# A four-layer network on one Trainium2 core: folding weights at the head of the third expert stage, first down products one slot later

## Chip, cores and metric

The kernel runs on 1 core of one Trainium2 chip. The metric is the device time of one execution in microseconds (us). Before the change it is 2271.5 us, the median of 3 runs (2271.24 to 2273.16).

## What is computed

The reference sends 16 sequences of 56 tokens of width 256 (896 tokens in all) through four layers. Each layer adds a gated cross attention over a context of 1500 rows, and then a gated feed-forward part. Those of layers 0, 2 and 3 are mixtures of experts. The part around the change is the feed-forward part of layer 2, the third of the four feed-forward stages, with 16 experts of which each token takes 6:

```
x = x + tanh(g_xattn[2]) * L2_attention(layernorm(x), context)
h = layernorm(x)
scores = softmax(h @ gate_w.T);  cw = the 6 largest scores of each token, else 0
y = sum over e of cw[:, e] * ((silu(h @ w_gate[e].T) * (h @ w_up[e].T)) @ w_down[e].T)
x = x + tanh(g_ffn[2]) * y
x = x + tanh(g_xattn[3]) * L3_attention(layernorm(x), context)
```

The attention of layer 3 has weights of its own for each of 16 heads (`Wq`, `w_kc_q`, `W_qr`, `W_kr`, `w_kc_kv`, `Wo`). The kernel multiplies them together ahead of the attention ("folds" them), two heads at a time, so that each query is one product with a folded matrix.

## The kernel before

The program is a row of stages. At the end of each, all five instruction queues meet (`stage_end`, semaphore `stage_met`). Every fp32 product is done as three products of high and low parts (`split_pairs`: high by high, high by low, low by high), so that one 128x128 by 448 product is three matmuls of 448 columns, written by line 922. Tokens are taken in two halves of 448.

**The third feed-forward stage** (`FFN[2]`) has 22 blocks of 128 hidden units (16 experts of 176). The order of its work is one hand-built list of tasks, made by `expert_order(22, side)` and walked by all five queues; each takes from it the tasks that are its own. A slot `k` stands for one block and one half of the tokens. In slot `k` the list has:

- `up`: TensorE multiplies the normalised tokens `YH`, `YL` with the gate and the up weights of the block (`WH`, `WL`), 12 matmuls into two banks of psum; ScalarE takes silu of the first (`R`, line 1933) and VectorE multiplies by the second (`HF`, line 2658). The `up` of slot 0 is done in the stage before.
- `gate`: VectorE multiplies `HF` by the tokens' gate for the block's expert (`GB`, line 2673), ScalarE makes the high part (`HH`, line 1956) and GpSimd the low part (`HL`, line 2201). `R`, `HF`, `HH` and `HL` are rings of 4 tiles, so the `HH` of slot `k` waits for the down product of slot `k - 4`.
- `down`: TensorE multiplies `HH`, `HL` with the down weights, 6 matmuls that are added up in banks 0 to 3 of psum over the whole stage. In the steady state slot `k` has the `down` of slot `k - 3`.
- one step of `side`, the folding for the next layer's attention, made by `fold_order(3, 1)`. Its first step is the load of the first pair's weights (`fload`), and then there are four steps a pair: `fu` (line 1180, from `WqrT`; ScalarE copies the result to `U`, line 1708), `fm` (line 1186, from `WoT` and `Wv`; to `MH`, line 1711, and `ML`), `fg` (`U` by `WcT`; to `G`, line 1716) and `fa` (line 1200, `G` by `Wq`; to `AH` and `AL`). There is one set of buffers for these weights, so pair `p + 1` is loaded behind pair `p`.
- `split`: ScalarE and GpSimd make the high and low parts of a coming block's weights (`WH` line 1926, `WL` line 2185) from `WS`, which SP has loaded (`fetch`, line 1052; four buffers).

The products of `up` and of the folding steps go through banks 4 to 7 in turn (`upper_uses`): each use waits until the result four uses back has been taken out. So the first half of `up` of slot 5 waits for `u_set`, ScalarE's copy of the first `fu`.

**The gates** are there only in slot 2: VectorE works the routing out (`route`), TensorE turns it, VectorE copies it to `GT`, SP writes it to DRAM (`gates_scratch`, line 1058), waits until it is there, and then reads it back broadcast, the gates of three blocks in six issues (`gload`, line 1063). SP issues in program order, and waits in that order too. The folding weights of pair 0 (lines 981 to 991, in `sp_fold`) and the `fetch` of block 5 stand behind these six.

Of the kernel before, what the change touches and what calls it, by code (L numbers as in the profile page):

```python
# [20 lines left out]
H = 16  # L21
# [6 lines left out]
NB0, NB2, NB3 = E0 + 4, E2 * I2 // P, E3 + 1  # L28
# [134 lines left out]
def expert_order(blocks, side):  # L163

    slots = [(n, c) for n in range(blocks) for c in range(2)]
    order, free = [("fetch", n) for n in range(4)] + [("split", 0), ("split", 1), ("route", 0)], FFN_FREE[2 if blocks == NB2 else 3]
    side = list(side)
    for k in range(len(slots) + 3):  # L170
        if k < len(slots):
            n, c = slots[k]
            if c == 0 and 4 <= n + 3 < blocks:
                order.append(("fetch", n + 3))
            order.append(("up", n, c))
        if k in (0, 2):
            order.append(("route", 1 + k // 2))
            if k == 2:
                order += [("gload", n) for n in range(free, free + 3)]
        for x in {0: (), 1: (), 2: (), 3: (0,), 4: (1, 2), 5: (3, 4, 5)}.get(k, (k,)):  # L180
            if x < len(slots):
                n, c = slots[x]
                order.append(("gate", n, c))
                order += [("gload", n + 3)] if c == 1 and free <= n < blocks - 3 else []
        for x in {4: (0,), 5: (1, 2)}.get(k, (k - 3,) if k > 5 else ()):
            order.append(("down", *slots[x]))
            if slots[x] == (blocks - 1, 0):
                order += [t for step in side for t in step]
                side = []
                order.append(("back", 0))  # L190
        if k < len(slots):
            n, c = slots[k]
            if side and k >= 2:
                order += side.pop(0)
            if c == 1 and n + 2 < blocks:
                order.append(("split", n + 2))
    return order + [("back", 1)] + ([("make", mt, 0) for mt in range(4, H // 2)] if blocks == NB2 else [])


def folding_ahead():  # L200
# [139 lines left out]
def bit_order(fold):  # L340
# [3 lines left out]
    for k in range(NT + 5):  # L344
# [19 lines left out]
FFN_FREE = {0: NB0 - E0, 2: 0, 3: NB3 - E3}  # L364
SWIGLU = {0: False, 2: True, 3: True}
CORES, CORE0 = {n: core_order(n != 2) for n in (1, 2, 3)}, core0_order()
FFN = {0: sparse_order(context_order(), folding_ahead()),
       2: expert_order(NB2, fold_order(3, 1)),
       3: expert_order(NB3, [])}
FFN1_FOLD = fold_order(2, 1)  # L370
FFN1 = FFN1_FOLD[0] + bit_order(FFN1_FOLD[1:])
# [2536 lines left out]
```

## Time and profile before

| | |
|---|---|
| median of 3 runs | 2271.5 us |
| the profiled execution's own time | 2275.43 us |
| its span in the trace | 2273.6 us |
| mean granted clock of TensorE | 0.97 of full |
| TensorE (PE) busy | 2143.3 us, 94% |
| VectorE (DVE), GpSimd (POOL), ScalarE (ACT) busy | 1541.5, 1478.2, 1035.6 us |
| chain that ended last, share on PE | 81% |
| moved by DMA | 160.14 MB, 70 GB/s mean |

Times in the trace are us from the start of the span, so the profiled execution's own time is 1.83 us more than its span. An engine's busy time is the union of its instructions; idle time matters only on the engine that the others wait for. The granted clock is a share of TensorE's full 2.4 GHz: 1.00, or 0.50 at 1.2 GHz. The third feed-forward stage lies from about 1507 to 1704 us.

### The profile page before, as it was taken

To read this page: it belongs to the slowest core of one execution; us is meant where nothing else is said; L and a number is where in the kernel's file an instruction comes from. 1 tells how busy PE (TensorE), PEld (TensorE's weight loads), DVE (VectorE), ACT (ScalarE), POOL (GpSimd) and SP (SyncE) were. 2 spreads that over 40 slices of the span, in tenths; PEclk is the share of its full clock that TensorE was granted. 3 is DMA by queue.
4 is the path that set the end of the run, shared out by engine and by line. 5 is a ranking of instruction groups with operands and counts; after the bars stand their busy time and mean duration, and the time that the engine had idled before them with its cause. 6 is when DMAs were issued, how large, how long until landed. Compare 5 with 4: busy or idle time off the path is not lost.

```text
span 2273.6 us, 30616 instructions
## 1 busy us (share of the span) xinstructions
PE 2143.3 (94%) x11232; PEld 1518.3 (67%) x11236; DVE 1541.5 (68%) x2492; ACT 1035.6 (46%) x1533; POOL 1478.2 (65%) x933
## 2 busy tenths in 40 slices
PE   7797999999999997898999999979998999999988
PEld 5586777766666664665666666568896666666588
DVE  6766763588887857666787888643335787888653
ACT  4452333555555545212555555434435555555443
POOL 0356763488888874465888888724443888888744
PEclk9899999999999999898999999989999999999989
DMA  3126865211111104001111111025421111111022
GB/s 93 43 76 195 258 225 153 63 54 41 42 51 52 28 29 131 24 1 42 41 53 50 41 41 48 8 77 155 139 85 55 41 48 55 41 42 48 2 65 81
DMA packets 60640, 160.14 MB, mean 70 GB/s; under 512 B 9669, under 2 KB 19669, under 8 KB 60108
## 3 DMA queue, kind: packets, MB, share of 16 engines
q1 hardware_dynamic: 60108, 157.86, 23.1%
q8 instruction: 90, 1.47, 0.3%
q10 hardware_dynamic: 384, 0.33, 0.1%
q14 instruction: 58, 0.48, 0.1%
HBM read 143.18 MB, written 14.98 MB: 70 GB/s over the span
## 4 chain that ended last, share of the span: by engine, by line
PE 81%; DVE 6%; ACT 3%; POOL 3%; issue 2%; DMA 2%; SPq 1%; ACTq 0%; PEldq 0%; DVEq 0%; POOLq 0%; PEld 0%
PE psum L1425 20%; PE psum L922 19%; PE psum L1415 10%; PE psum L1396 10%; PE psum L1417 10%; PE psum L1442 2%; PE psum L1579 2%; PE psum L1536 1%; PE psum L1302 1%; DMA kt_scratch<-kt 1%; POOL CL L1870 1%; PE psum L1180 1%; PE psum L1200 1%; POOL rstd L2100 1%; PE psum L1276 1%
## 5 line engine op out<-in xcount | busy, mean ns | idle before, releaser
L1848 ACT ACTIVATE E<-psum 125x896 f32<-125x896 f32 x576 | 527.8, 919 | 574.8 <-PE psum L1417 547.9
L2416 DVE TENSOR_REDUCE mx<-psum 128x1 f32<-128x500 f32 x945 | 611.7, 675 | 166.6 <-PE psum L1396 164.4
L2150 POOL TENSOR_TENSOR SA<-SA,E 125x896 f32<-125x896 f32 x282 | 597.3, 2118 | 22.1
L1425 PE MATMUL psum<-E,V 125*64 125x448 f32 x2304 | 472.0, 544 | 0.0
L1415 PE MATMUL psum<-Q,K 128*125 128x448 f32 x1152 | 332.0, 369 | 2.3 <-ACT E L1848 2.3
L1396 PE MATMUL psum<-K,Q 128*128 128x500 f32 x945 | 329.1, 402 | 2.6 <-ACT Q L1835 2.2
L1417 PE MATMUL psum<-Q,K 128*125 128x448 f32 x1152 | 330.3, 368 | 0.0
L1425 PEld LDWEIGHTS psum<-E,V 125*64 125x64 f32 x2304 | 171.5, 136 | 214.0 <-issue 202.5
L2150 POOL TENSOR_TENSOR SA<-SA,SB 125x896 f32<-125x896 f32 x93 | 194.1, 2087 | 148.8 <-DVE SB L2439 148.8
L1396 PEld LDWEIGHTS psum<-K,Q 128*128 128x128 f32 x945 | 174.7, 188 | 134.3 <-issue 34.6
L1415 PEld LDWEIGHTS psum<-Q,K 128*125 128x125 f32 x1152 | 213.3, 187 | 37.1 <-ACT E L1848 6.9
L1417 PEld LDWEIGHTS psum<-Q,K 128*125 128x125 f32 x1152 | 214.8, 186 | 21.8
L2201 POOL TENSOR_TENSOR HL<-HF,HH 128x448 fp32r<-128x448 f32 x70 | 81.0, 1161 | 136.6 <-ACT HH L1956 136.6
L2443 DVE RECIPROCAL RS<-psum 128x448 f32<-128x448 f32 x48 | 142.0, 2958 | 25.5 <-PE psum L1442 25.5
L2439 DVE TENSOR_TENSOR SB<-E,E 125x896 f32<-125x896 f32 x96 | 121.0, 1260 | 28.4 <-ACT E L1848 28.4
L2150 POOL TENSOR_TENSOR SA<-E,E 125x896 f32<-125x896 f32 x48 | 102.2, 2130 | 46.8 <-ACT E L1848 46.8
L2658 DVE TENSOR_TENSOR HF<-R,psum 128x448 f32<-128x448 f32 x62 | 38.3, 621 | 138.9 <-PE psum L922 122.2
L2211 POOL TENSOR_SCALAR S<-slot_of_t,slots 128x896 fp32r<-128x896 bf16 x32 | 88.3, 2766 | 47.6 <-DMA slot_of_t<-slots_scratch 31.6
L2131 POOL TENSOR_TENSOR Q<-QR,Q 64x448 fp32r<-64x448 f32 x96 | 109.3, 1139 | 11.8 <-POOL SA L2150 7.1
L1835 ACT ACTIVATE Q<-QR 64x448 fp32r<-64x448 f32 x192 | 110.5, 575 | 3.6 <-ACTq L930 0.3
L922 PE MATMUL psum<-YH,WH 128*128 128x448 f32 x264 | 104.1, 394 | 2.4 <-DVEq L930 2.4
L922 PE MATMUL psum<-YL,WH 128*128 128x448 f32 x264 | 99.8, 378 | 0.0
(299 smaller groups left out, 3588.9 us busy)
## 6 DMA issues: line engine op xcount, KB each, us to landing
K<-kt_scratch SPq DMA_DIRECT2D x48, 750.0 KB, 4.9
K<-kt_scratch SPq DMA_DIRECT2D x48, 375.0 KB, 5.9
EW<-in_f_w SPq DMA_DIRECT2D x64, 256.0 KB, 8.1
kt_scratch<-kt SPq DMA_DIRECT2D x16, 750.0 KB, 8.1
WS<-in_f_w SPq DMA_DIRECT2D x31, 384.0 KB, 4.7
GB<-gates_scratch SPq DMA_DIRECT2D x36, 224.0 KB, 3.9
slot_of_t<-slots_scratch SPq DMA_DIRECT2D x64, 112.0 KB, 4.5
WoT<-in_a_WoT SPq DMA_DIRECT2D x24, 256.0 KB, 3.2
```

Source lines behind the costliest of these rows:

```text
L922: i = e.matmul(o, a, b, start=start and n == 0, stop=stop and n == len(pairs) - 1, **kw)
L1396: e.matmul(psum[:, bank, 0:CW], Q1n[b % 3][:, tok(j)], K1t[b % 3][:, c * CW:(c + 1) * CW], start=True, stop=True).then_inc(small_made.sem, 1)
L1415: e.matmul(psum[0:LP, pair + c, 0:HT], K1t[b % 3][:, cols], Q1n[b % 3][:, half[c]], start=True, stop=False)
L1417: i = e.matmul(psum[0:LP, pair + c, 0:HT], K2t[b % 2][:, cols], Q2n[b % 2][:, half[c]], start=False, stop=True)
L1425: i = e.matmul(psum[c * DC:(c + 1) * DC, 4 + b % 2, 0:HT], V[0:LP, b, k * DC:(k + 1) * DC], E[g[n, b, k] % NE][0:LP, half[c]], start=k == ...
L1835: i = e.activation(high, raw, ACT.Copy)
L1848: e.activation(E[m % NE][0:LP, :].rearrange("p (c q) -> p c q", c=2), psum[0:LP, pair:pair + 2, 0:HT], ACT.Exp).then_inc(exp_set.sem, 1)
L2131: e.tensor_tensor(low, raw, high.bitcast(F32), ALU.subtract).then_inc(*(pool_own.up() if odd == 0 else (q2_set.sem, 1)))
L2150: e.tensor_tensor(SA[b % 2][0:LP, :], a[0:LP, :], x[0:LP, :], ALU.add).then_inc(sum_set.sem, 1)
L2416: e.tensor_reduce(mx[:, b % 2, j * 3 + c:j * 3 + c + 1], psum[:, bank, 0:CW], AX.X, ALU.max).then_inc(small_free.sem, 1)
L2439: e.tensor_tensor(SB[list(PAIRED).index(k)][0:LP, :], e0, e1, ALU.add).then_inc(pair_set.sem, 1)
L2443: e.reciprocal(RS[:, :], psum[:, bank, 0:HT]).then_inc(small_free.sem, 1)
```

## The change

```diff
--- before.py
+++ after.py
@@ -165,8 +165,11 @@
 
 
     slots = [(n, c) for n in range(blocks) for c in range(2)]
-    order, free = [("fetch", n) for n in range(4)] + [("split", 0), ("split", 1), ("route", 0)], FFN_FREE[2 if blocks == NB2 else 3]
-    side = list(side)
+    side, merged = list(side), blocks == NB2
+    order, free = side.pop(0) if side else [], FFN_FREE[2 if merged else 3]
+    order += [("fetch", n) for n in range(4)] + [("split", 0), ("split", 1), ("route", 0)]
+    downs = {5: (0,), 6: (1, 2, 3)} if merged else {4: (0,), 5: (1, 2)}
+    steady = max(downs)
     for k in range(len(slots) + 3):
         if k < len(slots):
             n, c = slots[k]
@@ -182,7 +185,7 @@
                 n, c = slots[x]
                 order.append(("gate", n, c))
                 order += [("gload", n + 3)] if c == 1 and free <= n < blocks - 3 else []
-        for x in {4: (0,), 5: (1, 2)}.get(k, (k - 3,) if k > 5 else ()):
+        for x in downs.get(k, (k - 3,) if k > steady else ()):
             order.append(("down", *slots[x]))
             if slots[x] == (blocks - 1, 0):
                 order += [t for step in side for t in step]
@@ -190,11 +193,11 @@
                 order.append(("back", 0))
         if k < len(slots):
             n, c = slots[k]
-            if side and k >= 2:
+            if side and k >= 3:
                 order += side.pop(0)
             if c == 1 and n + 2 < blocks:
                 order.append(("split", n + 2))
-    return order + [("back", 1)] + ([("make", mt, 0) for mt in range(4, H // 2)] if blocks == NB2 else [])
+    return order + [("back", 1)] + ([("make", mt, 0) for mt in range(4, H // 2)] if merged else [])
 
 
 def folding_ahead():
```

For the stage with 22 blocks (`merged`) it does two things. The first step of `side`, the load of the first pair's folding weights, goes to the head of the list, ahead of the routing; the steps behind it start at slot 3 in place of 2, and since the one that stood in slot 2 is gone from there, `fu` stays in slot 3, `fm` in slot 4 and so on. And the first `down`s come later: slot 5 has that of slot 0, slot 6 those of slots 1, 2 and 3, and from slot 7 on all is as before. For the last expert stage (9 blocks, no `side`) nothing changes. The weight loads of the second attention's queries, which are spread over four groups of heads (`heads_in`, four sets of issues between folding loads of the second feed-forward stage), are in both kernels as they are.

No queue has more or fewer instructions. On ScalarE, VectorE and GpSimd the instructions and their order are those of before; only SP and TensorE have another order, at one place each. Lines of `after` are higher by 3.

**SP at the head of the stage**, before: `WS` are the block weights, `GT` the gates, `GB` their broadcast copies, and the five `in_a_` loads the folding weights of pair 0. Names in brackets are the semaphores waited for.

```order
L1052 DMA WS_305<-in_f_w 128x768 [waits wl_set,wh_set,stage_met]
L1058 DMA gates_scratch<-GT_346 16x896 [waits gt_set]
L1063 DMA GB_322<-gates_scratch 64x896 [waits dma_gates_out0]
...
L1063 DMA GB_324<-gates_scratch 32x896
L981 DMA WqrT_349<-in_a_WrT 64x512
L984 DMA WoT_347<-in_a_WoT 128x512
L985 DMA Wv_348<-in_a_Wv 128x128
L990 DMA Wq_350<-in_a_Wq 128x512
L991 DMA WcT_352<-in_a_WcT 96x512
L1052 DMA WS_306<-in_f_w 128x768 [waits wl_set,wh_set]
```

The same place in the changed kernel:

```order
L984 DMA WqrT_349<-in_a_WrT 64x512 [waits stage_met]
L987 DMA WoT_347<-in_a_WoT 128x512
L988 DMA Wv_348<-in_a_Wv 128x128
L993 DMA Wq_350<-in_a_Wq 128x512
L994 DMA WcT_352<-in_a_WcT 96x512
L1055 DMA WS_305<-in_f_w 128x768 [waits wl_set,wh_set]
L1061 DMA gates_scratch<-GT_346 16x896 [waits gt_set]
L1066 DMA GB_322<-gates_scratch 64x896 [waits dma_gates_out0]
...
L1066 DMA GB_324<-gates_scratch 32x896
L1055 DMA WS_306<-in_f_w 128x768 [waits wl_set,wh_set]
```

The five folding loads, which stood behind the six `GB` issues, stand first, and wait only for the meeting of the queues. The `fetch` into `WS_305` comes behind them, and the one into `WS_306` directly behind the `GB`s.

**TensorE in slots 3 to 6**, before, by the first matmul of each product. `YH` by `WH_311` is `up` of slots 4 and 5, `WH_312` that of slot 6; `HH_329` to `HH_332` are the `down`s of slots 0 to 3.

```order
L1180 MATMUL psum<-WqrT_349 96x64 [waits dma_fold_r0,gt_set]
...
L922 MATMUL psum<-YH_50,WH_311 128x448 [waits gt_set,wl_set]
...
L922 MATMUL psum<-HH_329,WH_309 128x448 [waits hl_set]
...
L1186 MATMUL psum<-WoT_347,Wv_348 64x256 [waits dma_fold_m0,prod_set]
...
L922 MATMUL psum<-YH_50,WH_311 128x448 [waits u_set]
...
L922 MATMUL psum<-HH_330,WH_309 128x448 [waits hl_set]
...
L922 MATMUL psum<-HH_331,WH_310 128x448 [waits hl_set]
...
L922 MATMUL psum<-U_353,WcT_352 128x64 [waits u_set,dma_fold_a0,prod_set]
...
L922 MATMUL psum<-YH_50,WH_312 128x448 [waits ml_set,wl_set]
...
L922 MATMUL psum<-HH_332,WH_310 128x448 [waits hl_set]
...
L1200 MATMUL psum<-G_351,Wq_350 128x64 [waits g_set,prod_set]
```

And in the changed kernel:

```order
L1183 MATMUL psum<-WqrT_349 96x64 [waits dma_fold_r0,gt_set]
...
L925 MATMUL psum<-YH_50,WH_311 128x448 [waits gt_set,wl_set]
...
L1189 MATMUL psum<-WoT_347,Wv_348 64x256 [waits dma_fold_m0,prod_set]
...
L925 MATMUL psum<-YH_50,WH_311 128x448 [waits u_set]
...
L925 MATMUL psum<-HH_329,WH_309 128x448 [waits hl_set]
...
L925 MATMUL psum<-U_353,WcT_352 128x64 [waits u_set,dma_fold_a0,prod_set]
...
L925 MATMUL psum<-YH_50,WH_312 128x448 [waits ml_set,wl_set]
...
L925 MATMUL psum<-HH_330,WH_309 128x448 [waits hl_set]
...
L925 MATMUL psum<-HH_331,WH_310 128x448 [waits hl_set]
...
L925 MATMUL psum<-HH_332,WH_310 128x448 [waits hl_set]
...
L1203 MATMUL psum<-G_351,Wq_350 128x64 [waits g_set,prod_set]
```

The `down` of slot 0 moved from between `up` of slot 4 and `fm` to behind `up` of slot 5, and those of slots 1 and 2 from slot 5 to slot 6. The four folding steps and the `up`s stand in the same order as before.

## Rows read from the trace of the kernel before

**Rows 1.** The page, busy time by engine.

```profile
PE 2143.3 (94%) x11232; PEld 1518.3 (67%) x11236; DVE 1541.5 (68%) x2492; ACT 1035.6 (46%) x1533; POOL 1478.2 (65%) x933
```

**Rows 2.** Windows: span, busy us by engine (count), clock, DMA share, GB/s.

```profile
1530.00:1700.00 170.00, 170.00 (x909) 151.50 (x909) 57.54 (x95) 67.56 (x129) 80.86 (x59) 0.99 0.44 128
```

**Rows 3.** TensorE's waits, 1510 to 1530: who for whom, us, times, longest.

```profile
PE psum L1180 <- DMA WqrT<-in_a_WrT: 9.8, 1, 9.8
```

**Rows 4.** The chain, 1514 to 1530: start, us, what.

```profile
1516.90 1.80 DMA gates_scratch<-GT
...
1521.88 6.06 DMA WqrT<-in_a_WrT
```

**Rows 5.** Timeline of SP's queue, 1505 to 1525: start, us, issue.

```profile
1507.55 0.33 SPq L1052 DMA_DIRECT2D WS<-in_f_w  x1
1516.90 0.33 SPq L1058 DMA_DIRECT2D gates_scratch<-GT  x1
1518.72 3.12 SPq L1063 DMA_DIRECT2D GB<-gates_scratch  x6
...
1524.51 0.37 SPq L1052 DMA_DIRECT2D WS<-in_f_w  x1
```

**Rows 6.** Timeline of TensorE, 1528 to 1560: start, us, operation, idle before.

```profile
1528.08 1.51 PE L1180 MATMUL psum<-WqrT 64*96 64x64 f32 x8 [9.83 <-DMA WqrT<-in_a_WrT]
1529.51 0.74 PE L922 MATMUL psum<-YH,WH 128*128 128x448 f32 x1
...
1535.56 0.65 PE L1186 MATMUL psum<-WoT,Wv 128*64 128x256 f32 x4
1536.14 0.47 PE L922 MATMUL psum<-YH,WH 128*128 128x448 f32 x1
...
1541.97 0.45 PE L922 MATMUL psum<-YH,WH 128*128 128x448 f32 x1
...
1544.53 0.36 PE L922 MATMUL psum<-HH,WH 128*128 128x448 f32 x1
...
1545.74 1.00 PE L1200 MATMUL psum<-G,Wq 128*128 128x64 f32 x8
1546.55 0.45 PE L922 MATMUL psum<-YH,WH 128*128 128x448 f32 x1
```

**Rows 7.** Timeline of VectorE, 1516 to 1530, where it waits for the gates.

```profile
1523.78 0.63 DVE L2673 TENSOR_TENSOR HF<-HF,GB 128x448 f32<-128x448 f32 x1 [4.81 <-DMA GB<-gates_scratch]
```

**Rows 8.** Timeline of ScalarE, 1516 to 1533.

```profile
1524.43 0.58 ACT L1956 ACTIVATE HH<-HF 128x448 fp32r<-128x448 f32 x1 [6.81 <-DVE HF L2673]
1529.62 0.38 ACT L1708 ACTIVATE U<-psum 96x256 f32<-96x256 f32 x1 [4.61 <-PE psum L1180]
```

**Rows 9.** Timeline of GpSimd, 1516 to 1532.

```profile
1525.09 1.13 POOL L2201 TENSOR_TENSOR HL<-HF,HH 128x448 fp32r<-128x448 f32 x1 [10.47 <-ACT HH L1956]
```

**Rows 10.** Windows of one us around the wait, columns as in rows 2.

```profile
1509.00:1510.00 1.00, 1.00 (x5) 0.88 (x4) 0.04 (x1) 0.97 (x3) 0.00 (x0) 0.50 0.77 295
1520.00:1521.00 1.00, 0.00 (x0) 0.00 (x0) 0.00 (x0) 0.00 (x0) 0.00 (x0) 0.86 0.75 262
1533.00:1534.00 1.00, 1.00 (x4) 0.87 (x3) 0.00 (x0) 0.00 (x0) 0.00 (x0) 0.50 0.00 0
1534.00:1535.00 1.00, 1.00 (x5) 0.92 (x5) 0.55 (x2) 0.00 (x0) 0.00 (x0) 0.82 0.00 0
```

**Rows 11.** TensorE, first matmul after an idle of three us, in an earlier stage.

```profile
291.43 0.47 PE L1579 MATMUL psum<-S,YDH 128*128 128x448 f32 x1 [3.11 <-DVE YDL L2703]
```

**Rows 12.** TensorE, first matmul after an idle of three us, in a later stage.

```profile
2175.28 0.44 PE L1168 MATMUL psum<-ident,Y 128*128 128x128 f32 x2 [3.01 <-DVE Y L2521]
```

**Rows 13.** Windows just behind those two idles, columns as in rows 2.

```profile
292.00:295.40 3.40, 3.40 (x12) 2.93 (x11) 1.76 (x2) 0.34 (x1) 1.49 (x2) 0.51 0.72 235
2176.00:2179.50 3.50, 3.50 (x19) 3.50 (x18) 2.04 (x8) 2.00 (x6) 2.38 (x5) 0.51 0.00 0
```


## The prediction

> **What bounds the kernel now.** First the page: TensorE is busy for 94% of the span [rows 1], so it is the engine to follow, and a change pays where TensorE stands still. The windows of the third feed-forward stage say this more sharply: from 1530 to 1700 it is busy for 170 of 170 us [rows 2]. Whatever TensorE gains ahead of 1530 therefore moves the end of the stage by as much, unless a new wait takes it back. The table of TensorE's waits has one large wait ahead of that point, 9.8 us for `WqrT`, the first folding weights [rows 3]. The chain says why these are late: the gates' write to DRAM takes 1.80 us from 1516.90, the six broadcast reads follow, and `WqrT` is asked for only at 1521.88 and takes 6.06 us more [rows 4]. SP's own timeline shows that its queue is empty of issues between 1507.55 and 1516.90 [rows 5]: it stands waiting for the gates, with the folding loads behind, though these need nothing but a free buffer. On TensorE the idle ends at 1528.08 after 9.83 us, so it began at 1518.25 [rows 6].
>
> The wait has a second price. The granted clock is 1.00 until the idle, falls during it (0.86 on average in the microsecond from 1520), and is 0.50, the 1.2 GHz level, until after TensorE works again; it comes back within the microsecond from 1534, whose mean is 0.82 [rows 10]. With 0.36 us of that one at half, TensorE worked at half clock from 1528.08 to 1534.36, 6.3 us, which would have taken 3.1 at full clock. So the stall costs 9.8 of idle and 3.1 of slow work.
>
> **The change part by part.** *The load at the head.* Five issues move from behind the `GB` reads to the stage's start. They take SP from 1521.84 (1518.72 + 3.12) to 1524.51, 2.6 us [rows 5]. Now they run from 1507.55 to 1510.2. What they are moved past: the `fetch` into `WS_305` is asked for at 1510.2 in place of 1507.55 and is used only when block 4 is split, in slot 5, after 1530; its cover is 20 us against a landing of 6 [rows 4]. The gates' write waits for `GT` until 1516.90, and SP is free by then. The `GB` reads keep their place, and the `fetch` into `WS_306` comes 2.6 us earlier. In bytes, the tiles of the order rows give 0.92 MB of folding weights and 0.39 MB for `WS_305`; the queue moved 295 GB/s in the microsecond from 1509 [rows 10], so all are there after 4.4 us of transfer, near 1514 with the start of the first. `fu` at 1518.25 waits for nothing.
>
> *What is late next.* `fu`, `up` of slot 4 and `fm` now follow each other: 0.81 (a folding step, 1545.74 to 1546.55), 2.56 (12 matmuls, 1541.97 to 1544.53) and 0.58 (1535.56 to 1536.14) [rows 6], together 3.95, so `fm` is done at 1522.20. Then the first half of `up` of slot 5 waits for `u_set`, the copy of `fu`'s result. On ScalarE that copy stands behind the first `HH`, whose `HF` VectorE makes at 1523.78, when the gates have landed [rows 7]; the gates' path is as before. `HH` runs from 1524.43 for 0.58, the copy takes 0.38 [rows 8], so `U` is there at 1525.39. TensorE idles for 3.2 us in place of 9.83.
>
> *The `down`s.* Moving them removes nothing; it is cover. The low part of slot 0's `HH` is ready at 1526.2 (1525.09 + 1.13) [rows 9]; with the old order that `down` would have held TensorE in slot 4, with the new one it comes at 1527.95 and is ready. The path from `U` on: `up` 2.56, `down` 1.21 (1544.53 to 1545.74 [rows 6]), `fg` 0.81, `up` 2.56, three `down`s 3.63, `fa` 0.81, together 11.6. `fa` ends at 1537.0, against 1546.55 before: 9.6 us earlier. The pieces agree: 9.83 - 3.2 + 3.1 = 9.7. The bunched `down`s make ScalarE wait too: `HH` of slot 5 needs slot 1's `down`, which now ends at 1533.7; with it and the copy to `G` behind it (no more than 0.58 + 0.38) `G` is there at 1534.7, and `fa` comes at 1536.2. That leaves 1.5 us, so I cost it at nothing.
>
> *The clock after the new idle.* Its price lies between nothing and the 3.1 us of the old, longer idle. The nearest rows are two other idles, of 3.11 and 3.01 us, which end at 291.43 and 2175.28 [rows 11, 12]. The windows that begin 0.6 and 0.7 us behind them have a mean clock of 0.51 over 3.4 and 3.5 us, with TensorE busy throughout [rows 13]: the clock fell, and such a stretch costs half its length, 1.7. I take 1.7, with both ends in the range.
>
> Sum: 9.6 - 1.7 = 7.9. The profiled execution took 2275.4 us (a span of 2273.6 and 1.8 around it), so it would take 2267.5. The median of the runs is 3.9 lower, 2271.5, and gives **2263.6 us**.
>
> **The rivals.**
> (a) *The clock holds* through the new idle. For it: the idle is a third of the old one, and dense work stands on both sides. Against: rows 11 to 13. Then 2271.5 - 9.6 = 2261.9.
> (b) *No new wait*: the copy of `U` is not late, or the gates land earlier. The whole 9.8 + 3.1 would go, 2258.6. Against: ScalarE's order is unchanged, and the gates' write starts at the same 1516.90.
> (c) *The gain is partly given back by the bunched `down`s*: ScalarE's chain of `HH`, `G`, the next block's `WH` and `R` runs out of its 1.5 us and TensorE waits in slots 6 to 8, for 1 to 3 us in all: 2264.6 to 2266.6.
> (d) *The gates are late instead*: the head's loads crowd the queue and the gates' round trip runs behind them. Each microsecond is lost in full, since VectorE, `HH`, `U` and TensorE hang on it. From 3.4 us late on, the gain is below 4.5 us and not told from no change.
> (e) *Slower*, by the same place carried further: a backlog that keeps the gates' write and reads until 12.4 us later, from which point it is slower by over 4.5 us. That is 1.31 MB in the 21.7 us from 1507.6 to 1529.3, 60 GB/s. The row with a queue at work shows 295 [rows 10], and on average the stage's DMA engines are busy for 0.44 of the time [rows 2].
>
> The rule that speaks against this change is on the queue. The Trainium skill (DMA: Bandwidth & Descriptors, "Queues, rings and completion order") says that each DMA engine takes a ring's descriptors in order, so that later issues of SP stand behind earlier ones. By it the five loads delay whatever follows them: at the measured rate the head is empty before 1516.90 and the sum stays 2263.6, and at 60 GB/s it is rival (e), 2276. The trace agrees on the order's effect: `WqrT` itself, behind six gate reads, took 6.06 us.
>
> **How the numbers follow.** A difference below 0.2%, 4.5 us, can't be told from none here; so faster means below 2267.0. My forecast (a fallen clock) has 0.50, (a) 0.27, (b) 0.04, (c) 0.10, (d) 0.06, (e) 0.03. Faster is the first four, 0.91; same is (d), 0.06; slower is (e), 0.03. The range holds the forecast, (a) and (c), 0.87, less what single runs scatter: downwards from 2261.9 by 1.7, one half-clock stretch elsewhere that may come or go when everything behind is shifted, 2260.2; upwards to the end of (c), 2266.6.
>
> **What would show it.** In the new trace: the folding loads issued from about 1507.5; no wait of TensorE for `WqrT`; `fu` at about 1518.2; one idle of 3.2 us, ended by ScalarE's `U`, in front of `up` of slot 5; a half-clock stretch of 3.4 us near it (forecast) or none (a); the first gates multiplied by VectorE at 1523.8 as before; `fa` of pair 0 done near 1538.7 (or 1537.0), and TensorE without a gap from there to the end of the stage. An idle in slots 6 to 8 ended by ScalarE is (c). Gates multiplied after 1527 are (d) or (e). The forecast is wrong if TensorE finds another wait between 1518 and 1540 of more than 2 us, or if what the stage gains is lost behind its end.

## The result, and the profile after

The changed kernel takes 2266.05 us (median of 12 runs, 2264.34 to 2272.69), the kernel before beside it 2272.19 (median of 12, 2270.87 to 2276.8). The ratio is 0.9972, 95% interval [0.9962, 0.9983]: 3.9 to 8.6 us faster. In a later comparison (the run `after_again` below) the ratio is 0.9966 [0.9949, 0.9983], with medians of 2266.66 (12) and 2274.8 (18). The kernel before has medians of 2272.19, 2276.5, 2275.51 and 2274.8 in the four comparisons of this study, so a microsecond is taken as settled below only where a stretch of the trace shows it.

Lines of `after` are higher by 3. The span is 2267.5 us, TensorE busy for the same time as before [rows 1]:

```profile
PE 2143.3 (95%) x11232; PEld 1518.6 (67%) x11236; DVE 1540.9 (68%) x2492; ACT 1035.3 (46%) x1533; POOL 1481.4 (65%) x933
```

TensorE's waits from 1500 to 1560 (who for whom, us, times, longest): the wait for `WqrT` [rows 3] is gone, and one for `U` has come.

```profile
PE psum L925 <- ACT U L1711: 2.6, 1, 2.6
```

SP's queue, for [rows 5]. The five loads are issued from 1508.22 (the first two and the last are shown), before the queue stands waiting for the gates:

```profile
1508.22 0.48 SPq L984 DMA_DIRECT2D WqrT<-in_a_WrT  x1
1508.74 0.59 SPq L987 DMA_DIRECT2D WoT<-in_a_WoT  x1
...
1510.32 0.43 SPq L994 DMA_DIRECT2D WcT<-in_a_WcT  x1
1510.86 0.37 SPq L1055 DMA_DIRECT2D WS<-in_f_w  x1
1517.57 0.32 SPq L1061 DMA_DIRECT2D gates_scratch<-GT  x1
1519.41 3.12 SPq L1066 DMA_DIRECT2D GB<-gates_scratch  x6
```

Their transfers, with the `WS` load behind them: the queue moves data from 1509 to 1516 at 187 GB/s on average and is then empty (windows, columns as in rows 2). The last of them, `WS`, has landed 5.7 us behind its issue at 1510.86, 1.0 us ahead of the gates' write at 1517.57 (DMA issues: KB, us from issue to landing).

```profile
1509.00:1516.00 7.00, 6.22 (x27) 5.17 (x26) 5.16 (x28) 4.68 (x6) 1.96 (x1) 0.84 0.65 187
1516.00:1517.50 1.50, 1.50 (x11) 1.38 (x10) 1.50 (x3) 0.00 (x0) 0.00 (x0) 1.00 0.00 0
```

```profile
WS<-in_f_w SPq DMA_DIRECT2D x1, 384.0 KB, 5.7
```

TensorE's timeline, for [rows 6]: `fu`, `up` of slot 4, `fm`, the idle ahead of `up` of slot 5, `down` of slot 0, `fg`, `up` of slot 6, the three `down`s, `fa`, and the next `up`.

```profile
1518.84 0.89 PE L1183 MATMUL psum<-WqrT 64*96 64x64 f32 x8
1519.66 0.47 PE L925 MATMUL psum<-YH,WH 128*128 128x448 f32 x1
...
1522.26 0.65 PE L1189 MATMUL psum<-WoT,Wv 128*64 128x256 f32 x4
1525.51 0.74 PE L925 MATMUL psum<-YH,WH 128*128 128x448 f32 x1 [2.60 <-ACT U L1711]
...
1530.15 0.57 PE L925 MATMUL psum<-HH,WH 128*128 128x448 f32 x1
...
1532.11 1.00 PE L925 MATMUL psum<-U,WcT 96*128 96x64 f32 x8
...
1535.48 0.36 PE L925 MATMUL psum<-HH,WH 128*128 128x448 f32 x1
...
1539.14 1.00 PE L1203 MATMUL psum<-G,Wq 128*128 128x64 f32 x8
1539.95 0.45 PE L925 MATMUL psum<-YH,WH 128*128 128x448 f32 x1
```

VectorE, and then ScalarE, for [rows 7, 8]: the gates' product, and behind it `HH`, the late copy `U`, and the later `HH` (which waits for a `down`) with `G`.

```profile
1523.95 0.63 DVE L2676 TENSOR_TENSOR HF<-HF,GB 128x448 f32<-128x448 f32 x1 [4.31 <-DMA GB<-gates_scratch]
```

```profile
1524.61 0.58 ACT L1959 ACTIVATE HH<-HF 128x448 fp32r<-128x448 f32 x1 [6.31 <-DVE HF L2676]
1525.09 0.36 ACT L1711 ACTIVATE U<-psum 96x256 f32<-96x256 f32 x1
...
1536.95 0.58 ACT L1959 ACTIVATE HH<-HF 128x448 fp32r<-128x448 f32 x1 [3.71 <-PE psum L925]
1537.43 0.26 ACT L1719 ACTIVATE G<-psum 128x128 f32<-128x128 f32 x1
```

Windows of the clock, for [rows 10] and [rows 2] (columns as there). The clock falls at the end of the idle, near 1524.9, and is back within the microsecond from 1531, whose mean of 0.64 puts 0.72 us of it at half: TensorE works at half from 1525.51 to 1531.72, 6.2 us. From 1540 on it has no gap.

```profile
1524.00:1525.00 1.00, 0.00 (x0) 0.00 (x0) 0.58 (x1) 0.39 (x1) 0.00 (x0) 0.95 1.10 215
...
1531.00:1532.00 1.00, 1.00 (x5) 0.89 (x4) 1.00 (x2) 0.00 (x0) 0.61 (x1) 0.64 0.69 190
```

```profile
1540.00:1697.00 157.00, 157.00 (x849) 140.22 (x849) 53.58 (x88) 62.04 (x119) 73.08 (x54) 1.00 0.42 124
```

**The measure used below.** The stage does not start at the same time in two executions: its first matmul is at 1507.58 before and at 1508.25 after. So the runs are compared by a stretch, F: from the end of `up` of slot 3 (where `fu` could start) to the first matmul behind `fa`. Before it is 1546.55 - 1518.25 = 28.30 us; after it is 1539.95 - 1518.84 = 21.11. The change gains 7.2 us there. From that matmul to the end of the span it is 727.05 before (2273.6 - 1546.55) and 727.6 after (2267.5 - 1539.95): nothing is given back that the scatter of this rest (725.9 to 729.2 over all runs) does not hold. Each run has one profile, and F varies too: the second profile of the changed kernel (`after_again`) has 19.62, 1.5 less, nearly all of it by the length of the slow stretch.

### The profile page after: what moved, and what is told of

The parts are those of the page before. It is cut to its first block, busy times and chain, and to the rows that moved or that the text cites. A ratio compares the mean times of both kernels' runs of the same rounds, so it can differ in the third digit from the quotient of the medians.

```text
span 2267.5 us, 30616 instructions
## 1 busy us (share of the span) xinstructions
PE 2143.3 (95%) x11232; PEld 1518.6 (67%) x11236; DVE 1540.9 (68%) x2492; ACT 1035.3 (46%) x1533; POOL 1481.4 (65%) x933
## 4 chain that ended last, share of the span: by engine, by line
PE 80%; DVE 6%; POOL 3%; ACT 3%; issue 3%; DMA 2%; SPq 1%; ACTq 0%; PEldq 0%; DVEq 0%; POOLq 0%; PEld 0%
PE psum L1428 20%; PE psum L925 19%; PE psum L1418 10%; PE psum L1399 10%; PE psum L1420 10%; PE psum L1445 2%; PE psum L1582 2%; PE psum L1539 1%; PE psum L1305 1%; POOL CL L1873 1%; DMA kt_scratch<-kt 1%; PE psum L1183 1%; POOL S L2214 1%; PE psum L1203 1%; POOL rstd L2103 1%
```

## The experiments

All medians are of timed runs beside the kernel before on the same chip. "Idles" are TensorE's inside F, with what ended them; behind a clock of 0.50 stands how long TensorE worked at it.

| run | F, us | idles in F | clock in F | median (runs) | ratio to before, 95% |
|---|---|---|---|---|---|
| before | 28.30 | 9.83 `WqrT` | 0.50, for 6.3 us of work | | |
| after | 21.11 | 2.60 `U` | 0.50, for 6.2 us of work | 2266.05 (12) | 0.9972 [0.9962, 0.9983] |
| load_only | 22.82 | 4.16 `HL` | 0.50, for 6.3 us of work | 2267.3 (6) | 0.9958 [0.9944, 0.9971] |
| downs_only | 28.11 | 9.52 `WqrT` | 0.50, for 6.6 us of work | 2275.68 (12) | 0.9996 [0.9986, 1.0005] |
| filled_after | 19.15 | 0.71 `U`, 0.45 `ML` | 1.00 | 2268.84 (8) | 0.9965 [0.9953, 0.9977] |
| act_later | 18.69 | 0.73 `HL`, 1.92 `ML` | 1.00 | 2266.81 (9) | 0.9959 [0.9944, 0.9973] |
| copies_ahead | 17.34 | 0.74 `HL`, 0.27 `R` | 1.00 | 2265.2 (6) | 0.9963 [0.9948, 0.9977] |
| filled_before | 26.27 | 1.46 `WqrT` | 1.00 | 2272.94 (10) | 0.9998 [0.9984, 1.0012] |
| loads_between | 24.07 | 2.14 `WqrT`, 3.70 `U` | 0.50, for 5.6 us of work | 2270.25 (10) | 0.9976 [0.9962, 0.999] |
| pair1_ahead | 17.36 | 0.77 `HL`, 0.25 `R` | 1.00 | 2264.53 (7) | 0.9949 [0.9931, 0.9966] |
| after_again | 19.62 | 2.40 `U` | 0.50, for 3.4 us of work | 2266.66 (12) | 0.9966 [0.9949, 0.9983] |

### load_only and downs_only: the two halves of the change

load_only is the changed kernel with the old order of the `down`s, downs_only the kernel before with the new one.

```diff
-    downs = {5: (0,), 6: (1, 2, 3)} if merged else {4: (0,), 5: (1, 2)}
+    downs = {4: (0,), 5: (1, 2)}
```

```diff
-        for x in {4: (0,), 5: (1, 2)}.get(k, (k - 3,) if k > 5 else ()):
+        downs = {5: (0,), 6: (1, 2, 3)} if blocks == NB2 else {4: (0,), 5: (1, 2)}
+        for x in downs.get(k, (k - 3,) if k > max(downs) else ()):
```

> The loads of pair 0 at the head, the downs in their old slots. Measure: the head stretch, from the first matmul of the stage to the first matmul behind the first fa; 38.97 us before the change, 31.70 with it. My theory (the moved downs are cover only): the down of slot 0 now stands in slot 4 and waits for the low part that GpSimd made at 1526.4, 0.9 us after TensorE went on in the changed kernel, with fm (0.6) still to do: head stretch 33.2, the whole 1.5 us above the changed kernel, 4.5 to 5 below before. Rival 1 (the moved downs bring nothing): 31.7, as the change. Rival 2 (the moved downs are what brings the gain): 38 or more.

> The downs moved, the loads behind the gates' reads as before. My theory: TensorE waits for WqrT as before and nothing else is late there: one idle of 9.8 us ended by WqrT, head stretch 39.0, no difference from before. Rival (the moved downs are what brings the gain): head stretch 32 to 34 and about 6 us below before.

load_only has F 22.82, 5.5 us better than before and 1.7 worse than the change. Its slow work is as long as in that profile of the change (6.3 against 6.2 us), so the 1.7 are in the main the longer idle (4.16 against 2.60). Its TensorE timeline shows the idle in slot 4, ahead of the `down` of slot 0, for the low part that GpSimd makes once the gates are there:

```profile
1523.97 0.74 PE L925 MATMUL psum<-HH,WH 128*128 128x448 f32 x1 [4.16 <-POOL HL L2204]
```

downs_only has F 28.11 against 28.30, and a ratio of 0.9996. So the load at the head makes the gain, and the moved `down`s are cover for the gates' path: alone worth nothing, with the load 1.7 us of the 7.2. (The medians of load_only and of the change do not tell these 1.7 us apart.)

### filled_after and filled_before: what the clock costs

Both add matmuls whose results nobody reads, to keep TensorE at work in the idle: 10 behind the first `fm` of the changed kernel (shown), 46 in front of the first `fu` of the kernel before.

```diff
+                if f == 2 and (kind, t[1]) == ("fm", 0) and 10:
+                    for r in range(10):
+                        e.matmul(psum[:, 0, 0:HT], m["WH"][1][:, 0:P], YH[:, 0, half[0]], start=True, stop=True)
```

> The changed kernel with ten more matmuls of 448 columns into a bank that nothing reads, right behind the first fm, so that TensorE works in most of the idle of 2.6 us (extra work, no other use). My theory (the idle has a second price through the granted clock): the clock stays at 1.00 there, the idle is 0.5 us, TensorE goes on at the same time relative to the stage's start, and the head stretch is 3.1 us shorter, 28.6; the whole 3 us below the changed kernel. Rival (the clock's fall has to do with the stage's start or the load of the DMA queues and not with the idle, or the half-speed work costs nothing because others wait anyway): the clock falls all the same, or the stretch stays 31.7.

> The kernel before with 46 more matmuls of 448 columns into a bank that nothing reads, in front of the first fu, so that TensorE works through most of the 9.8 us of waiting for WqrT (extra work, no other use). It takes the two prices of the old wait apart. My theory: the wait's end is set by SP's queue and stays where it is, TensorE then goes on at a clock of 1.00 in place of 0.50, and F is 28.3 - 3.1 = 25.2. Rival 1 (half-speed work costs nothing there, since the gates' path holds TensorE back anyway): F stays above 27.5. Rival 2 (the clock falls for another reason): 0.50 around fu all the same.

With the idle filled the clock stays at 1.00 (windows of filled_after around it, columns as in rows 2):

```profile
1521.00:1539.00 18.00, 16.84 (x90) 14.73 (x90) 7.73 (x11) 6.84 (x14) 10.60 (x8) 1.00 0.66 194
```

In filled_before the clock stays at 1.00 too. `fu` comes later than in the kernel before (10.7 us behind `up` of slot 3, of which 1.46 idle, against 9.83), since `WqrT` took 6.9 us from issue to landing in place of 6.1; so F is 26.27 where 25.2 were expected. But from `fu` to the first matmul behind `fa` it takes 1540.51 - 1524.95 = 15.56 us at full clock in place of 1546.55 - 1528.08 = 18.47. That is 2.9 us for 6.3 of slow work, a little under the half (TensorE's first line behind the wait and the one behind `fa`, then the window):

```profile
1524.95 0.86 PE L1180 MATMUL psum<-WqrT 64*96 64x64 f32 x8 [1.46 <-DMA WqrT<-in_a_WrT]
...
1540.51 0.45 PE L922 MATMUL psum<-YH,WH 128*128 128x448 f32 x1
```

```profile
1514.00:1541.00 27.00, 25.55 (x139) 22.98 (x137) 7.47 (x12) 7.69 (x15) 10.67 (x8) 1.00 0.65 166
```

Why it is less than half stands in the changed kernel's own timeline, in the 2nd and the 12th matmul of one `up` at full clock, and the same two of the next at half:

```profile
1519.97 0.36 PE L925 MATMUL psum<-YL,WH 128*128 128x448 f32 x1
...
1521.97 0.36 PE L925 MATMUL psum<-YH,WL 128*128 128x448 f32 x1
...
1526.05 0.58 PE L925 MATMUL psum<-YL,WH 128*128 128x448 f32 x1
...
1529.78 0.58 PE L925 MATMUL psum<-YH,WL 128*128 128x448 f32 x1
```

A matmul every 0.200 us (2.00 / 10) against every 0.373 (3.73 / 10): the slow one costs 0.173 of 0.373, 46% of the time spent. So 6.3 and 6.2 us of slow work cost 2.9 each. In filled_after F falls by 2.0 (21.11 to 19.15) in place of 2.9: TensorE resumes 0.3 us later against `fu` (1526.28 - 1519.30 = 6.98, in the change 6.67), since the gates came later, and a wait of 0.45 us for `ML` appeared that the slow clock had hidden. Neither median shows these 2 us: filled_after's ratio, 0.9965, lies inside the interval of the change, and the interval of filled_before holds 1.

### act_later and copies_ahead: whose wait is the new one

The new idle is ended by `U`. Its copy needs nothing of the gates, but ScalarE's order has it behind the first `HH`, which does. In act_later ScalarE takes the gated slot 0 (`HH`) behind the copy `U` and the `R` of slot 4. In copies_ahead `MH` and `ML` are also made earlier, on ScalarE and on VectorE.

```diff
-        for kind, *t in FFN[f]:
+        for kind, *t in moved(FFN[f], ("gate", 0, 0), ("up", 2, 0)) if f == 2 else FFN[f]:
```

```diff
-        for kind, *t in FFN[f]:
+        if f == 2:
+            ahead = moved(moved(FFN[f], ("fm", 3, 0), ("up", 2, 0)), ("gate", 0, 0), ("fm", 3, 0))
+        for kind, *t in ahead if f == 2 else FFN[f]:
...
-        for kind, *t in FFN[f]:
+        for kind, *t in moved(FFN[f], ("fm", 3, 0), ("up", 1, 1)) if f == 2 else FFN[f]:
```

(`moved(order, task, behind)` puts one task right behind another; the last line is VectorE's.)

> The changed kernel with one move on ScalarE: the HH of slot 0, which waits for the gates, stands behind R of slot 4 in place of in front of the copy to U. My theory (the new wait is ScalarE's order, behind it the gates' path): no wait for U; up of slot 5 runs at once, then TensorE waits about 1.1 us for the low part of slot 0 and 1.5 us for ML in front of up of slot 6; the two short idles leave the clock at 1.00; up of slot 6 starts 21.9 us after the stage's first matmul (24.7 in the changed kernel) and the head stretch is 28.9; the whole 2.8 us below the changed kernel. Rival 1 (U is late for another reason): the wait for U stays, 31.7. Rival 2 (the clock falls all the same): one us or less is gained, 30.7 to 31.7.

> As act_later, and on ScalarE and VectorE the copy of the first fm (MH, ML) too stands ahead of the first products that wait for the gates. Measure F: from the end of up of slot 3 to the first matmul behind the first fa; 28.3 us before the change, 21.1 with it, 22.8 in load_only, 19.2 in filled_after, 18.7 in act_later. My theory (what is left in the stretch is the order of copies behind the gates): no wait for U, none for ML; one wait of 0.7 us for the low part of slot 0; the clock stays at 1.00; F 16.8 to 17.3, the whole 4 us below the changed kernel, if the other stages ran alike (their scatter is larger than that). Rival (another wait takes ML's place, that for R of slot 5 or for slot 1's low part): F stays at 18 to 18.7, with an idle in front of or within up of slot 6.

In act_later `U` is copied 5.3 us earlier (counted from the stage's first matmul), and the wait for it is gone; the next two in the row are then to be seen on TensorE. ScalarE, and TensorE:

```profile
1520.63 0.38 ACT L1711 ACTIVATE U<-psum 96x256 f32<-96x256 f32 x1 [1.50 <-PE psum L1183]
```

```profile
1527.12 0.47 PE L925 MATMUL psum<-HH,WH 128*128 128x448 f32 x1 [0.73 <-POOL HL L2210]
1531.36 0.45 PE L925 MATMUL psum<-YH,WH 128*128 128x448 f32 x1 [1.92 <-DVE ML L2306]
```

The two idles sum to as much as the one before (2.65 against 2.60), yet F falls by 2.4 us, since the clock stays at 1.00 (2.9 were to be had by the rates above; the other 0.5 was not traced). In copies_ahead the wait for `ML` goes too and F is 17.34, 3.8 us better than the change. Against the second profile of the change, with its short slow stretch, act_later and copies_ahead gain 0.9 and 2.3 us. The medians do not show these gains: the ratios of 0.9959 and 0.9963 are not told from the change's 0.9972 and 0.9966. Part of what copies_ahead gains in F is given back behind it: the second pair's `WqrT` is issued where SP's order has it, behind the gates of the next blocks, and is now late. TensorE:

```profile
1540.84 0.86 PE L1183 MATMUL psum<-WqrT 64*96 64x64 f32 x8 [1.71 <-DMA WqrT<-in_a_WrT]
```

### loads_between: the queue rule, measured

The kernel before with the new order of the `down`s, and the five loads issued between the gates' write and SP's wait for it, so that they stand directly ahead of the gate reads (at their old place they are left out).

```diff
                     e.dma_start(GS[f - 2, ...], m["GT"][...]).then_inc(gs_out.sem(f), 16)
+                    if f == 2:
+                        sp_fold(e, 3, 0)
                     e.wait_ge(*gs_out.at(f))
```

> The moved downs, and the five loads of pair 0 asked for between the gates' write and their reads: the worst place for them by the order of the queue. Measure: from the first GB issue to VectorE's first product with the gates; 5.06 us before the change, 4.54 with it. If what is asked for first is moved first (my theory, and what makes the head of the stage the right place), the reads stand behind 0.92 MB, some 2 us of which are not yet moved when they are asked for: 6.0 to 7.5 us, with the reads asked for 1.2 us later besides; U comes 2 to 3 us later than with the change and F is 23 to 24.5. Rival (the reads share the DMA engines with what is ahead of them and the gates' round trip hardly notices): 5.1 us or less and F 22 or less.

SP, then VectorE:

```profile
1520.16 0.33 SPq L1059 DMA_DIRECT2D gates_scratch<-GT  x1
1520.54 0.48 SPq L982 DMA_DIRECT2D WqrT<-in_a_WrT  x1
...
1523.11 3.12 SPq L1066 DMA_DIRECT2D GB<-gates_scratch  x6
```

```profile
1529.85 0.62 DVE L2677 TENSOR_TENSOR HF<-HF,GB 128x448 f32<-128x448 f32 x1 [7.61 <-DMA GB<-gates_scratch]
```

From the first gate read's issue to VectorE's product it is 6.74 us (1529.85 - 1523.11), and from the write to the product 9.69. The change, whose loads are long through by then, has 4.54 and 6.38, and in the other nine profiles the first is 4.33 to 5.06. So issues of the same queue that stand directly ahead delay the reads by some 2 us, and by another 1 us through SP's own time for issuing. This is the rule that the prediction drew on (the Trainium skill, DMA: Bandwidth & Descriptors, "Queues, rings and completion order"), and the run agrees with it. What speaks for the order, and not for an even sharing of the engines, is that the loads themselves were not held up by the reads behind them: `WcT`, the last, landed 4.5 us behind its issue, against 5.2 in the change, where only `WS` is behind it. The DMA issues of loads_between, then of the change:

```profile
WcT<-in_a_WcT SPq DMA_DIRECT2D x1, 192.0 KB, 4.5
```

```profile
WcT<-in_a_WcT SPq DMA_DIRECT2D x1, 192.0 KB, 5.2
```

The order costs the change nothing, because its loads are issued seven microseconds ahead of the write and have landed by then.

### pair1_ahead and after_again: a further version, and the change once more

pair1_ahead is copies_ahead with the second pair's `WqrT`, `WoT` and `Wv` issued right behind the first six gate reads; `Wq` and `WcT` stay at their old place.

```diff
                 for rows, one_gate in gate_rows(f, x):
                     e.dma_start(m["GB"][x % 3][rows, :], ...).then_inc(gb_in.sem(f, n), 16)
+                if f == 2 and x == 2:
+                    sp_fold(e, 3, 1, "early")
```

> This is copies_ahead with one more edit on SP: three of the second pair's five folding loads (WqrT, WoT, Wv) are issued right behind the first six gate reads, near 1522, where they wait only for the first pair's fu and fm; before they stood behind the next six gate reads, at 1533.8, and the second fu waited 1.71 us for WqrT. Theory (the late issue alone makes that wait): the wait of 1.71 us is gone, the second fu follows its up directly, and the time from the first fa to the end of the span falls from 728.5 to about 726.8; the stretch up to the first fa stays near 17.3. Against the changed kernel that is 3.8 + about 0.8 better, so about 2263 on a chip where the change gives 2266 to 2267. Rival 1 (the three loads crowd the next six gate reads, which follow on the same queue): the block-3 gates come later than before and VectorE or TensorE waits for them instead, 1 us or more. Rival 2: the 1.71 us is replaced by another wait for the same folding (WcT or Wq, which are still loaded late), and the rest stays at 728.5.

> The changed kernel as it is, on the same chip as pair1_ahead, so that the two can be set side by side. Theory: 3.9 to 8.6 us faster than the kernel before, as in its first comparison, with the one wait for ScalarE's U of about 2.6 us and the half-clock stretch of about 6.8 us behind it; pair1_ahead is then about 4 us below it. Rival (the scatter between executions outweighs what the edits give): the two medians lie within 2 us of each other.

The wait is gone, F is as in copies_ahead (17.36), and the second `fu` follows its `up`. SP, then TensorE, of pair1_ahead:

```profile
1521.60 0.48 SPq L985 DMA_DIRECT2D WqrT<-in_a_WrT  x1
```

```profile
1539.09 0.89 PE L1186 MATMUL psum<-WqrT 64*96 64x64 f32 x8
```

From the first matmul behind `fa` to the end it is 727.5 us against 728.5 in copies_ahead, 1.0 less where 1.7 were expected. One place of the rest is a longer slow stretch behind the stage: from 1700 to 1720 the mean clock is 0.83 here and 0.91 in copies_ahead. Windows of pair1_ahead, then of copies_ahead:

```profile
1700.00:1720.00 20.00, 16.02 (x77) 13.61 (x75) 10.24 (x39) 12.04 (x26) 5.11 (x14) 0.83 0.11 38
```

```profile
1700.00:1720.00 20.00, 13.86 (x74) 11.96 (x75) 10.37 (x39) 12.32 (x26) 5.13 (x14) 0.91 0.11 38
```

The ratio of 0.9949 is the lowest of the study. Beside the change on the same chip its median is 2.1 us lower (2264.53 against 2266.66), but the intervals overlap ([0.9931, 0.9966] and [0.9949, 0.9983]): faster than the kernel before is shown, faster than the change is not, except in the stretch F. Some 4 us had been expected between the two, and 2.1 bear out neither that nor the rival's "within 2 us".

after_again is the changed kernel once more. Its wait is the same, its slow stretch half as long: within the microsecond from 1527 the clock falls, and it is back early in that from 1531.

```profile
1527.15 0.47 PE L925 MATMUL psum<-YH,WH 128*128 128x448 f32 x1 [2.40 <-ACT U L1711]
```

```profile
1527.00:1528.00 1.00, 0.85 (x3) 0.81 (x4) 0.00 (x0) 1.00 (x3) 1.00 (x1) 0.82 1.07 259
...
1531.00:1532.00 1.00, 1.00 (x6) 0.92 (x5) 0.23 (x1) 1.00 (x3) 0.99 (x1) 0.97 0.30 108
```

That is 3.4 us of slow work (1527.64 to 1531.06), a price of 1.6 at 46%, and F is 19.62: 8.7 us better than before.

## Why the prediction was right

The median, 2266.05, lies in the range, and the kernel is faster as forecast. The mechanism is the one forecast, but that the median lies inside is in part luck: it is 0.55 us below the upper end, 2266.6, which stood for rival (c), and (c) did not come. In the later comparison the median is 2266.66, a hair outside, while the gain by the ratio, 7.7 us, is nearer to the forecast's 7.9 than in the first, 6.4. Step by step:

- **The load at the head.** As said: no wait for `WqrT`, `fu` directly behind `up` of slot 3. load_only and downs_only show that this is the cause.
- **Past the gates.** As said: the write to DRAM is issued 9.32 us behind the stage's first matmul in both kernels (1516.90 - 1507.58, and 1517.57 - 1508.25), and VectorE's first product with the gates comes 15.7 us behind it, 16.2 before. Rivals (d) and (e), late gates and a backlog, fell with this, and loads_between shows that the mechanism exists and only the distance keeps it away. The distance is smaller than was worked out: the 1.31 MB were to be there after 4.4 us at 295 GB/s, near 1514, 2.9 us ahead of the write, and at 187 GB/s they took 7 us and landed 1.0 us ahead of it. The 295 was a single microsecond.
- **What is late next.** The right wait at the right place, 2.60 us in place of 3.2 (2.40 in the second profile). The term was 0.6 too large because everything was laid against the old trace: the gates' product came 0.5 us sooner behind the stage's start than there. It came as soon in downs_only (1531.70 - 1516.05 = 15.65), which has the old queue, so that is scatter and not the change. Rival (b), no new wait, fell; act_later shows that ScalarE's order makes the wait.
- **The `down`s.** Nothing by themselves, and cover with the load, as said. After the bunched `down`s ScalarE does wait 3.71 us for one, and is done with `G` at 1537.7, 1.4 us ahead of `fa` at 1539.14 (predicted: 1.5). TensorE has no idle in slots 6 to 8, so rival (c) fell.
- **The clock.** This is the term that was mis-sized: a slow stretch of 3.4 us at a price of 1.7 was forecast, and the first profile has 6.2 us of slow work, 2.9 by the measured rates. The two rows on which the price was built [rows 11 to 13] showed one length each; the second profile of the change shows that length, and load_only, loads_between and downs_only 5.6 to 6.6 us. The term is not one number but differs between executions of the same program. Both prices, 1.6 and 2.9, lie between the two ends that the prediction gave it, nothing and 3.1 us. Rival (a), the clock holds, came in neither profile.
- **The sum.** 7.9 us were predicted. The first profile has 7.2, and the pieces agree: 9.83 - 2.60 of idle, and 2.9 of slow work each time. Against the forecast's pieces that is 0.6 better by the idle, 1.2 worse by the new slow stretch and 0.2 by the old one; that the first two partly cancel is luck. The second has 8.7 (9.83 - 2.40 + 2.9 - 1.6). On the whole time the midpoints of the two ratios are 6.4 and 7.7 us of 2272. The median came 2.4 us above the forecast, of which 0.7 is the kernel before, which measured 2272.19 here against 2271.5; the remaining 1.7 is within what the interval leaves open.

## What to carry to other kernels

A queue that stands waiting for a round trip through memory is the place to look at first: whatever in it doesn't depend on the round trip can be issued ahead, at some distance, for directly ahead of the reads it delays them. When a long wait is taken away, ask whose program order puts the next result behind the same event: here a copy of 0.4 us behind the gates on ScalarE kept 2.6 of 9.8 us. Taking `HH` behind that copy shortened the stretch by 2.4 us against one profile of the change and by 0.9 against the other, with the clock at 1.00. And price an idle of TensorE as a range, from the shortest to the longest slow stretch that the traces show behind one (here 3.4 to 6.6 us of work).

## What the runs showed of the hardware that was not expected

The idle's size alone does not set the price. Behind 2.60 us TensorE worked slowly for 6.2 us, behind 2.40 us in another execution of the same kernel for 3.4 (there the clock fell only at 1527.64, 0.5 us after TensorE had gone on), behind 3.70 and 4.16 us for 5.6 and 6.3, and behind 9.83 us for 6.3. Two idles of 0.73 and 1.92 us with 2.3 us of work between them (act_later) cost none in the one profile that there is, and neither did one of 1.71 us (copies_ahead). The Trainium skill (TensorE: Matmul & The Clock Gate, "What's actually happening") says that how many matmuls run cold differs between runs of one kernel, since the hardware's watch on the engine's activity is not tied to the kernel's start. The two profiles of the change agree.

The same makes part of the scatter between executions, as far as can be estimated; this scatter is larger than most edits here are worth. Ahead of the stage the programs of all eleven profiles are the same, yet the stage's first matmul comes at 1503.6 to 1516.1. Added up from the trace, the clock is at half for 92 to 93 us ahead of it in five profiles, which start the stage at 1506.9 on average (1503.6 to 1510.1), for 99 to 100 in five others, at 1508.7 (1507.3 to 1510.4), and for 110 in downs_only, the last of all. Windows of downs_only, then of filled_before, the first of all:

```profile
400.00:600.00 200.00, 195.09 (x952) 130.93 (x950) 147.76 (x191) 102.89 (x138) 143.02 (x78) 0.98 0.17 51
...
800.00:1000.00 200.00, 173.78 (x936) 116.61 (x936) 126.12 (x262) 72.76 (x121) 108.13 (x93) 0.91 0.17 52
```

```profile
400.00:600.00 200.00, 195.55 (x957) 130.25 (x956) 151.91 (x196) 104.94 (x136) 149.72 (x81) 1.00 0.17 51
...
800.00:1000.00 200.00, 174.96 (x963) 118.53 (x967) 126.45 (x270) 72.07 (x122) 110.20 (x96) 0.93 0.17 52
```

Each 0.02 of a window is about 8 us at half clock, so these two places make most of the 17 between them; at 46% they would cost 8 of the 12.4 us by which the two starts differ, an estimate, since part of the time at half clock is idle. The other spread, some us each way, is not explained by the clock and was not followed up. It is why the verdicts above rest on the stretch F, and why two profiles of one kernel are worth more than one.
